# First FFN block of a one-layer language tower: the two scale-bound sums one slot later, W_down's splits from slot 10 and its Hadamard products from slot 12

## What is computed

```python
def ffn(x):                       # x: 4096 x 512, after a layer norm
    x = fwht(x * SU_ug) / 64
    up = x @ W_up.T * (Wscale_ug[:2048] * 64)
    gate = x @ W_gate.T * (Wscale_ug[2048:] * 64)
    x = silu(gate) * up           # 4096 x 2048
    x = fwht(x * SU_dp) / 64
    return x @ W_down.T * (Wscale_dp * 64)
```

## Time and profile before

| | us |
|---|---|
| runs (3) | 1321.51, 1324.57, 1324.11; median 1324.11 |
| profiled execution | 1321.03 |
| its span | 1319.1 |
| first block, slots 0 to 31 | 132.5 to 332.2 |
| PE busy | 1230.1 (93% of the span) |
| DVE busy | 659.0 (50%) |
| POOL busy | 574.0 (44%) |
| ACT busy | 418.5 (32%) |

### The profile page before, as it was taken

How to read it: one execution, slowest core, us unless ns; L and a number is a source line. 1 busy time by engine, 2 the same in 40 slices (tenths; PEclk the granted TensorE clock), 3 DMA queues, 4 the chain that set the end, 5 groups by cost and what they waited for, 6 DMA issues and landing times.

```text
span 1319.1 us, 18434 instructions
## 1 busy us (share of the span) xinstructions
PE 1230.1 (93%) x7065; PEld 586.0 (44%) x7065; DVE 659.0 (50%) x1136; ACT 418.5 (32%) x731; POOL 574.0 (44%) x487
## 2 busy tenths in 40 slices
PE   6765879889999999999999999999999999999999
PEld 3542334334444444444444444444444444444444
DVE  2778599655553635544554545454554454451110
ACT  5764675521242023311332133302331133212210
POOL 0652487411575237531764166523753176411210
PEclk9887889999999999999999999999999999999999
DMA  9800134542452344424533345234433353120000
GB/s 329 336 1 1 32 72 84 109 96 64 119 114 49 88 104 104 73 72 98 111 81 76 85 104 112 48 86 100 108 75 73 83 125 73 33 72 8 1 1 32
DMA packets 231043, 113.17 MB, mean 86 GB/s; under 512 B 209412, under 2 KB 210744, under 8 KB 230456
## 3 DMA queue, kind: packets, MB, share of 16 engines
q1 hardware_dynamic: 219776, 77.78, 27.0%
q0 software_dynamic: 10240, 33.56, 8.6%
q10 hardware_dynamic: 952, 0.75, 0.2%
HBM read 53.08 MB, written 9.70 MB: 48 GB/s over the span
## 4 chain that ended last, share of the span: by engine, by line
PE 75%; DVE 11%; DMA 4%; ACT 4%; issue 3%; POOL 3%; SPq 0%; DVEq 0%; ACTq 0%; POOLq 0%
PE bank L1370 23%; PE bank L1371 23%; PE bank L1372 23%; DMA prod<-sg 3%; PE bank L1528 3%; ACT xT L1110 1%; POOL p L517 1%; DMA xT<-in_L_tok_proj_weight 1%; DVE prod L870 1%; DVE wd L677 1%; PE bank L1569 1%; DVE h L665 1%; DVE a L1009 1%; DVE xT L917 1%; DVE h L932 1%
## 5 line engine op out<-in xcount | busy, mean ns | idle before, releaser
L1370 PE MATMUL bank<-xT,wgu 128*128 128x512 f16 x1024 | 391.4, 382 | 4.3 <-DVE a L1001 2.8
L1371 PE MATMUL bank<-xT,wgu 128*128 128x512 f16 x1024 | 391.3, 382 | 0.0
L1372 PE MATMUL bank<-xT,wgu 128*128 128x512 f16 x1024 | 391.0, 382 | 0.0
L568 POOL TENSOR_TENSOR hid<-a,hid 128x512 f16<-128x512 f32 x128 | 177.1, 1384 | 202.9 <-ACT hid L1110 202.4
L1001 DVE SCALAR_TENSOR_TENSOR a<-bank,kap,sg 128x512 f32<-128x512 f32 x128 | 96.0, 750 | 325.4 <-PE bank L1372 289.5
L1370 PE MATMUL bank<-wd,hid 128*128 128x512 f16 x512 | 195.4, 382 | 0.0
L1371 PE MATMUL bank<-wd,hid 128*128 128x512 f16 x512 | 195.4, 382 | 0.0
L1372 PE MATMUL bank<-wd,hid 128*128 128x512 f16 x512 | 195.1, 381 | 0.0
L1370 PEld LDWEIGHTS bank<-xT,wgu 128*128 128x128 f16 x1024 | 101.0, 99 | 124.6 <-issue 6.3
L1372 PEld LDWEIGHTS bank<-xT,wgu 128*128 128x128 f16 x1024 | 100.8, 98 | 123.0 <-issue 3.9
L1110 ACT ACTIVATE hid<-a 128x512 f16<-128x512 f32 x128 | 80.5, 629 | 233.7 <-DVE a L1001 233.5
(11 more groups left out here) (203 smaller groups left out, 1379.4 us busy)
## 6 DMA issues: line engine op xcount, KB each, us to landing
out<-a SPq DMA_DIRECT2D x24, 256.0 KB
wgu<-in_L_ffn_W_gate SPq DMA_DIRECT2D x4, 1024.0 KB, 15.2
wgu<-in_L_ffn_W_up SPq DMA_DIRECT2D x4, 1024.0 KB, 15.1
wd<-in_L_ffn_W_down SPq DMA_DIRECT2D x4, 1024.0 KB, 14.8
out<-h_row SPq DMA_DIRECT2D x8, 256.0 KB
hid<-att_table,ids_p POOLq DMA_INDIRECT x72, 3.5
xT<-in_L_tok_proj_weight SPq DMA_DIRECT2D x1, 1024.0 KB, 9.2
p<-in_L_attn_Wq SPq DMA_DIRECT2D x1, 1024.0 KB, 12.5
```

Source lines behind the costliest of these rows:

```text
L568: nc.gpsimd.tensor_tensor(hid[:, 1, s, :], a32[:, :], hid[:, 0, s, :], ALU.subtract)\
L1370: mm(dst, w[0], v[0], start=first, stop=False)
L1371: mm(dst, w[0], v[1], start=False, stop=False)
L1372: return mm(dst, w[1], v[0], start=False, stop=final)
```

## The change

Each step of the two scale chains that comes after its terms moves one slot later, on PE, DVE and POOL: the first sum and its reading from slot 2 to 3, `half_scale(1)` from 3 to 4; the second sum and its reading from slot 7 to 8, `split_scale` from 8 to 9, `fit_scale` from 9 to 10. The terms stay in slots 1 and 6, the heads' waits in slots 4 and 8. Of the splits the first (v = 0) moves from slot 9 to 10, v = 2 from 10 to 11, v = 4 from 11 to 12; the others stay. Of the Hadamard products v = 0 to 4, 6, 8, 10, 12 move one slot later; v = 4 is then the first that stands in slot 16, and uses bank 4.

```diff
-SPLIT_BESIDE = (9, 10, 10, 11, 11, 12, 12, 13, 13, 14, 14, 15, 15, 16, 16, 17)
-HADA_BESIDE = (11, 12, 13, 14, 15, 16, 16, 17, 17, 18, 18, 19, 19, 20, 21, 22)
+SPLIT_BESIDE = (10, 10, 11, 11, 12, 12, 12, 13, 13, 14, 14, 15, 15, 16, 16, 17)
+HADA_BESIDE = (12, 13, 14, 15, 16, 16, 17, 17, 18, 18, 19, 19, 20, 20, 21, 22)
@@ gpsimd
-                if s == BOUND_BESIDE + 1:
+                if s == BOUND_BESIDE + 2:
                     bound_power(1)
-                if s == FIT_BESIDE + 1:
+                if s == FIT_BESIDE + 2:
                     bound_power(2)
@@ vector
-                if s == BOUND_BESIDE + 1:
+                if s == BOUND_BESIDE + 2:
                     bound_low(1)
-                if s == BOUND_BESIDE + 2:
+                if s == BOUND_BESIDE + 3:
                     half_scale(1)
                 if s == FIT_BESIDE:
                     fit_terms()
-                if s == FIT_BESIDE + 1:
+                if s == FIT_BESIDE + 2:
                     bound_low(2)
-                if s == FIT_BESIDE + 2:
+                if s == FIT_BESIDE + 3:
                     split_scale()
-                if s == FIT_BESIDE + 3:
+                if s == FIT_BESIDE + 4:
                     fit_scale()
```

## The result

**1330.46 us** is the median of five runs (1328.13 to 1331.92). The kernel before, run beside it, took 1323.52 (1321.51 to 1324.57). The ratio is 1.0054 with an interval of 1.0041 to 1.0067: slower by about 7 us, more than the 0.3% that a measurement can tell. The prediction said 1322.6 and a range up to 1329. The kernel was run a second time among the experiments and gave 1331.21 beside 1322.81, ratio 1.0064 (1.0049 to 1.0078).

What follows compares the result with a forecast made beforehand. The prediction took DVE's chain of `a` to decide in slots 3 to 8 and PE to bound from the second block on. Its terms, -0.4 by slot 13 and -1.1 at slot 16, took 1324.1 to 1322.6 us; range 1316 to 1329.

Steps and rivals of the forecast that it cites:

- DVE is who is behind in slots 3 to 8: First block, slots 3 to 8: DVE runs almost without a gap, so the change is counted on its chain of `a`.
- First sum later: Slots 2 and 3: DVE no longer waits 2.84 us for the up half behind the sum; `a` of slot 3 2.9 us earlier.
- DVE's gap ahead of slot 7: Ahead of `a` of slot 7: DVE's one idle gap of 1.24 us goes, counted as -1.2 us.
- Slot 8: New PE wait for the bound's read, about 8 us, then half clock: `a` of slot 9 at 215.6, +1.7 us.
- Slots 9 to 13: Changed splits, scale steps and Hadamard products: +1.2 us in all by `a` of slot 11, -0.4 by that of slot 13.
- Slots 6 and 7: Second sum later: DVE's gap goes, -1.2 us, so `a` of slot 8 starts 4.1 us earlier, at 205.3.
- third rival: Slots 3 to 8: DVE's mixes escape POOL's work at the shared port, -5.2 us, 1317.4; chance 0.23.
- Slot 16 on: From slot 16: the stop between its two products goes, the entry waits instead; net -1.1 us by the first row sum.
- PE was the bound: Rival: both stops at the bound sums and their half clock go, only slot 8's comes; -8.5 us, 1315.6; chance 0.04.
- slower rival: DVE gains nothing by slot 8 and the new wait is not paid for: +4.2 us, 1328.3; chance 0.15.
- the lists do nothing: Rival: slots 9 to 13 only trade work and slot 16 alone is left; 1324.7, inside the forecast's band, no own chance.
- the forecast's own band: The forecast with unknowns of half clock at slot 12, mixes and slot 16: 1321.5 to 1326 us, chance 0.58.

Runs made afterwards that it cites:

- the two kernels with light POOL work: Before, and before with only the first sum later, each with POOL's lower halves beside slots 3 to 5 cut to 8 of 512 columns: 1323.81 and 1321.85 us.
- the sums alone: Kernel before with both sums one slot later on PE, DVE and POOL, and the old lists: 1325.97 us, ratio 1.003.
- the kernel with the lists alone: Kernel before with only the two new lists of splits and Hadamard products, both sums staying in slots 2 and 7: 1328.81 us, ratio 1.0051.
- the kernel with both sums behind: Kernel before with the first sum one slot later and the second in slot 7 but behind the up half, old lists: 1323.02 us, ratio 0.9992.

## Why the prediction was wrong

**What held.** *DVE is who is behind in slots 3 to 8.* PE's 13.8 us of stops went and came again as 12.3, and DVE's chain of `a` decided. *First sum later*: -2.9 predicted, -2.88 measured; the stop in slot 4 was to be 1.4 and was 1.5, and cost nothing. *DVE's gap ahead of slot 7*: 1.24 predicted, 1.29 gained from `a` of slot 6 to that of slot 7. *Slot 8*: a stop of about 8 was predicted, 10.8 measured, and `a` of slot 9 at +2.1 against +1.7. The 8 was a slip: from its own terms (`a` of slot 6 at 188.9, its 0.7 us, two halves of 2.59 and the sum) PE reaches the wait at about 195 and not 198, and stands 11 us. It came there at 197.3 in before's time, close to the 198 only because `a` of slot 6 was 0.7 early and not 2.9. `a` of slot 9 does not hang on this. *Slots 9 to 13*: +0.7 and -0.8 against +1.2 and -0.4, and no wait for a transpose of W_down. These are the DVE rows of after for slot 8; the stop is the idle time ahead of the second `a`, for PE comes back late with the up half:

```profile
209.29 0.73 DVE L1001 SCALAR_TENSOR_TENSOR a<-bank,kap,sg 128x512 f32<-128x512 f32 x1
209.94 0.14 DVE L690 TENSOR_SCALAR h<-bank 128x1 f32<-128x1 f32 x1
...
218.08 0.75 DVE L1001 SCALAR_TENSOR_TENSOR a<-bank,kap,sg 128x512 f32<-128x512 f32 x1 [4.17 <-PE bank L1372]
```

**Two sizes inside it were off and cancelled, which was luck.** In "Slots 6 and 7" `a` of slot 8 was to be 4.1 early and was 2.1. The term that was missing is the mixes: from `a` of slot 3 to that of slot 8 the sixteen instructions took 29.4 us before and took 31.4 in after:

```profile
L678 DVE SCALAR_TENSOR_TENSOR wd<-wd 128x1024 f32<-128x1024 f32 x8 | 16.5, 2062 | 0.3
L677 DVE TENSOR_TENSOR wd<-wd 128x1024 f32<-128x1024 f32 x8 | 14.9, 1860 | 0.1
```

I had costed the move of half_scale at nothing for "the same work". It was cover: its two 128x8 instructions stood beside POOL's work, and when it moved, mixes took the place. The Trainium skill (SBUF — State Buffer, "SBUF: two separate sides") says that DVE and GpSimd hold their shared port pair as an exclusive lock, the loser blocked for a whole instruction. The trace agrees as far as it goes: half_scale's instructions end with POOL's, a mix takes 1.21 us at its shortest and 2.06 beside POOL, and the two kernels with light POOL work agree in direction. Beside a mix both are stretched, since POOL's 128x512 subtraction also goes from 1.15 to about 2.1; that each waits in turn for the other would look like this, but no run here tells it from the two slowing one another in another way. My third rival had named this rule, with the wrong sign: it let mixes escape POOL where they ran into it. In the other direction, from `a` of slot 8 to that of slot 9 10.3 us were expected and 8.79 came, as the half clock behind the stop was shorter than after the old one. The stretch table of after during the stop, where DVE is busy for 10.86 of 11.00, and behind it, where the clock is 0.76 against the 0.50 of the earlier trace rows:

```profile
198.00:209.00 11.00, 1.36 (x7) 0.39 (x4) 10.86 (x8) 5.13 (x9) 10.68 (x6) 0.71 0.35 65
210.00:216.00 6.00, 5.85 (x66) 3.33 (x67) 2.03 (x8) 3.29 (x6) 2.64 (x3) 0.76 0.28 53
```

**The step that failed is "Slot 16 on".** It gave -1.1 us to all that follows slot 15; measured, from `a` of slot 15 to the second block, it is +5.8 (from -0.8 to +5.0). It has two faults. *Slot 16* was to give 1.1: the stop of 2.6 between the two products would go, and the wait at the entry would cost less. The stop went. The entry wait is 2.22 us, and the spell of half clock behind it took 5.27 us for twelve matmuls where before it had been 4.26, so +0.6 and not -1.1 from `a` of slot 15 to the row sum of slot 18. In the second execution of after the same twelve took 4.03 us and the distance was -0.7, so this term is decided by the clock of the execution more than by the change. This is the first matmul of the spell in after:

```profile
265.72 0.59 PE L1370 MATMUL bank<-wd,hid 128*128 128x512 f16 x1 [2.22 <-issue]
```

*Slots 17 to 23* had no term of their own at all. I counted that one product fewer was made by slot 15 and took the rest of the list as shifted. The list has two entries that land in slot 19 or later, those of products 10 and 12, and I followed neither on DVE's queue. There the slot of a product decides whether its lower half stands ahead of or behind 4.6 us of row work. The price is 2.83 us of stop and 1.7 us of half clock, 4.5; measured from one row sum to the next 4.7, and 4.3 to 4.7 in the other executions that have this stop.

Summed over the block of the profiled executions: -1.5 predicted, less 0.4 by slot 13, plus 1.7 for slot 16, plus 5.1 for the tail, is +4.9; measured +5.0. The 7.1 us of the profiled executions have another 2.05 from ahead of the first edited line. The medians lie 6.9 and 8.4 apart, so they too are some 2 us beyond the block. Whether that is an effect of the change is open. Counted from before, the zero of the five profiled executions with the second sum in slot 8 is 0.2, 1.2, 2.05, 2.5 and 4.0 us late, and that of the eight others 0.2 to 4.2, so it follows no edit; the profiled execution of before has the earliest of all, and lies 2.5 us below its median. I see no way for an edit to reach back there. The part of the 3 us of the sums alone beyond 1.9 is open as well.

**The rivals.** That PE was the bound fell: its stops came back as 12.3 us, and `a` went by DVE's chain. The slower rival gave 1328.3 and a chance of 0.15, near what came, but it was to decide from `a` of slot 8 later than 209 in before's time, and that stood at 207.2. The loss came elsewhere, so it was right in sign and wrong in mechanism. That the lists do nothing is refuted by the kernel with the lists alone. The forecast's own band was added up a little low: its unknowns give 1321.9 to 1326.3 around 1322.6, not 1321.5 to 1326, which changes nothing here.

## What to carry to other kernels

When a list of places is edited, follow each entry that changed on the queue of every engine that serves it, to the last entry, and ask of the consumer which work will now stand ahead of its producer. A short result that the bounding engine needs soon belongs ahead of long row work in an in-order queue: here that alone is worth 6.9 us, more than any move of the sums. Cheap instructions that stand beside another engine's heavy ones are cover, and moving them has a price.

## What of the hardware was unexpected

Stops of the same length were followed by different clocks. Before and the kernel with both sums behind have the same stop of 2.55 us ahead of line 1569; behind it the stretch tables show:

```profile
305.00:310.00 5.00, 3.15 (x15) 1.49 (x16) 1.67 (x4) 0.00 (x0) 1.06 (x1) 1.00 0.44 104
```

```profile
306.00:312.00 6.00, 4.24 (x13) 1.65 (x14) 1.57 (x4) 0.00 (x0) 1.02 (x1) 0.72 0.37 87
```

One stretch ran at full clock, the other partly at 1.2 GHz. The granted clock of one execution thus moves marks by up to 2.5 us at a stop of 2.2, and by 0.2 to 4.2 us before any edited line is reached; the second execution of after starts its second block 1.4 later than the first, counted inside the block. Distances of one execution are safe to about that much, which is why the experiments above were read by the place of a loss and not by its last microsecond.
